# Routed blocks of an audio tower: gate and up products in banks of their own, weights applied in PSUM, 99 blocks, a pair's rows in place

## The reference

```python
fwd = ewma(x); bwd = ewma(x reversed), reversed back      # carry = 0.1 * xi + 0.9 * carry
h = (fwd + bwd) / 2 @ W.T + b                             # 12000 tokens x 256
h = h + hidden_of_two_selective_scans(layernorm(h))       # state 64: softplus, exp, h_t = d_t * h_(t-1) + g_t
x2 = layernorm(h)
shared = (silu(x2 @ Gs.T) * (x2 @ Us.T)) @ Ds.T           # hidden 512
# 16 experts in 4 groups of 4: best 2 groups by the sum of their two best scores,
# in them the best 4 experts, w = their sigmoid scores over their sum
hw = silu(x2 @ gate_e) * (x2 @ up_e) * w_e                # hidden 64 for each expert
out = h + shared + sum over e of hw @ down_e
```

## Time and profile before

| | |
|---|---|
| median of 3 runs | 1447.79 us (1443.96 to 1449.68) |
| profiled execution | 1445.21 us, its span 1443.4 |
| mean granted TensorE clock | 0.916 of full speed |
| busy: PE, weight load, DVE | 1221.5, 1036.5, 997.5 us |
| busy: ACT, POOL | 559.2, 599.7 us |
| routed products, 512 columns (L1616) | 1272 matmuls |
| DVE scalings by token weight (L1397) | 848 x 276 ns |

### The profile page before, as it was taken

One profiled execution on the slowest core, in us unless ns is written; L12 is line 12 of the kernel. 1 busy time (PEld: TensorE's weight loads), 2 busy tenths in 40 slices (PEclk: granted clock), 3 DMA queues, 4 the chain that ended last, 5 costly groups with the idle time before them and its releaser, 6 DMA issues.

```text
span 1443.4 us, 22785 instructions
## 1 busy us (share of the span) xinstructions
PE 1221.5 (85%) x6476; PEld 1036.5 (72%) x6476; DVE 997.5 (69%) x2991; ACT 559.2 (39%) x925; POOL 599.7 (42%) x442
## 2 busy tenths in 40 slices
PE   4439948996899779996799879998699979999997
PEld 3328736884788658885688658886588868888886
DVE  6785895779548875779548885588647774665553
ACT  1523613651336423551235423463236523323332
POOL 2261163155422743146332635138341553265553
PEclk9559978998899999998899978998899999999999
DMA  3601112221221112221231112212122213123330
GB/s 73 154 27 58 32 25 79 48 45 37 39 71 41 32 43 56 68 43 33 47 81 41 32 37 43 70 38 42 37 63 49 46 42 69 40 37 58 48 36 9
DMA packets 86891, 71.00 MB, mean 49 GB/s; under 512 B 38654, under 2 KB 81471, under 8 KB 86776
## 3 DMA queue, kind: packets, MB, share of 16 engines
q0 software_dynamic: 23616, 25.52, 11.6%
q1 hardware_dynamic: 60928, 43.61, 10.6%
q10 hardware_dynamic: 2232, 0.42, 0.2%
HBM read 33.10 MB, written 39.52 MB: 50 GB/s over the span
## 4 chain that ended last, share of the span: by engine, by line
PE 56%; DVE 25%; issue 10%; POOL 3%; DMA 3%; ACT 2%; POOLq 0%; DVEq 0%; SPq 0%; ACTq 0%
PE gu_ps L1616 14%; PE gu_ps L1593 13%; PE d_ps L1674 9%; PE d_ps L1656 6%; DVE hid L1397 5%; PE ch_ps L1567 3%; PE ch_ps L1511 2%; PE ch_ps L1643 2%; DVE h L1404 1%; DVE h L1137 1%; DVE fw L1038 1%; DVE states L1115 1%; PE ch_ps L1635 1%; PE ch_ps L1521 1%; DVE ends L1030 1%
## 5 line engine op out<-in xcount | busy, mean ns | idle before, releaser
L745 POOL DMA_INDIRECT out_dram<-block_rows,entry x106 | 171.7, 1620 | 328.2 <-ACT block_rows L886 173.0
L1616 PE MATMUL gu_ps<-gu_hi,bx_hi 128*128 x424 | 193.0, 455 | 12.8 <-issue 12.7
L713 POOL DMA_INDIRECT lists<-listed,pos x96 | 131.8, 1373 | 164.7 <-DVE pos L1307 140.2
L1656 PE MATMUL d_ps<-down,hid 128*125 128x256 f32 x768 | 191.6, 395 | 0.0
L1397 DVE SCALAR_TENSOR_TENSOR hid<-gu_ps,entry,hid 128x64 f32<-128x64 f32 x848 | 171.7, 276 | 8.0 <-ACT hid L873 7.1
L1616 PE MATMUL gu_ps<-gu_hi,bx_lo 128*128 x424 | 176.1, 415 | 0.0
L1616 PE MATMUL gu_ps<-gu_lo,bx_hi 128*128 x424 | 175.4, 414 | 0.0
L1656 PEld LDWEIGHTS d_ps<-down,hid 128*125 128x125 f32 x768 | 147.9, 198 | 22.8
L873 ACT ACTIVATE hid<-gu_ps 128x512 f32<-128x512 f32 x106 | 63.4, 598 | 231.9 <-PE gu_ps L1616 231.8
L734 POOL DMA_INDIRECT block_rows<-token_rows,entry x106 | 112.5, 1061 | 64.5 <-issue 35.5
L1408 DVE TENSOR_TENSOR bx_lo<-ch_ps,bx_hi 128x256 fp32r<-128x256 f32 x106 | 44.6, 421 | 131.5 <-ACT bx_hi L880 127.9
(11 more groups left out here) (273 smaller groups left out, 3006.8 us busy)
## 6 DMA issues: line engine op xcount, KB each, us to landing
token_rows<-xn SPq DMA_DIRECT2D x24, 500.0 KB
out_dram<-h SPq DMA_DIRECT2D x24, 500.0 KB
t<-rstd_scratch SPq DMA_DIRECT2D x24, 250.0 KB, 4.0
x_in<-in_x_dram SPq DMA_DIRECT2D x15, 375.0 KB, 3.4
entry<-lists SPq DMA_DIRECT2D x106, 8.0 KB, 2.5
block_rows<-token_rows,entry POOLq DMA_INDIRECT x106, 2.8
out_dram<-block_rows,entry POOLq DMA_INDIRECT x106, 3.8
lists<-listed,pos POOLq DMA_INDIRECT x96, 2.7
```

The lines of the kernel that those rows point to most:

```text
L713: pool.indirect_dma_start(out=lists, out_offset=bass.IndirectOffsetOnAxis(pos[:, arg:arg + 1], 0), in_=listed[:, arg, :], in_offset=None). ...
L745: pool.indirect_dma_start(out=out_rows[0:there, :], out_offset=bass.IndirectOffsetOnAxis(entry[n % UE][:, ID:ID + 1].bitcast(U32), 0), in_ ...
L1616: last = pe.matmul(gu_ps[:, 2 * (g % 2) + q, :], a[n % 2][:, k, :], w[:, k, bass.ds(of, 1), :].rearrange("p g h -> p (g h)"), start=(k == ...
L1656: last = pe.matmul(d_ps[0:TP, j, :], hid[g % 4][:, tc], down[:, m, :], start=(m == 0 and j % 2 == 0), stop=(m == M - 1), skip_group_check= ...
```

## The change

- Blocks: each pair gives only as many as are sure to be full (`take`), 6, 12, 12, 11, 12, 12, 12 and 22: 99. A missing one leaves its slot empty of products; the first pair with blocks has them in its last six routed slots.
- `block_products`: first the gate columns of both groups, 256 each, into one bank, then the up columns into the other. `silu` follows the first half in the same slot on ACT; PE's first half waits for `silu_done` of two slots ago, its second for `hid_done`.
- `block_hidden`: one multiplication of the up bank by the eight weights in place in PSUM (at the start of the next slot), and one of silu by that.
- `h_tok` and `h2` become two buffers that pairs take in turn, with `y` in place. Routing has a scratch of its own (`route_t`).
- The class row uses 64 partitions for each sequence with a wait between them. The exponential's table is loaded ahead of the waits in `ssm_log` and `ssm_decay`.
- New due ticks; an `EARLY` table for the first two pairs; the splitting of the routed weights due at ticks 1.4 to 11.4.

```diff
 CHAIN = (
-    ("ewma", 0, dict(SP=-32.0, DVE=-30.5, POOL=-29.0, ACT=-28.5)),
-    ("ewma_back", 0, dict(DVE=-29.5)),
-    ("ewma", 1, dict(SP=-27.5, DVE=-28.5, POOL=-27.0, ACT=-26.5)),
+    ("ewma", 0, dict(SP=-32.0, DVE=-33.5, POOL=-29.0, ACT=-28.5)),
+    ("ewma_back", 0, dict(DVE=-32.0)),
+    ("ewma", 1, dict(SP=-23.5, DVE=-28.5, POOL=-27.0, ACT=-26.5)),
...
-    ("tok", 4, dict(PE=-24.5, DVE=-24.0)),
+    ("tok", 4, dict(PE=-25.0, DVE=-25.0)),
...
-    ("ln2_stats", 2, dict(DVE=-1.0, POOL=-0.5)),
+    ("ln2_stats", 2, dict(DVE=0.5, POOL=-2.0)),
...
-    ("list", 0, dict(POOL=15.0)),
+    ("list", 0, dict(POOL=12.5)),
...
-    ("table", 2, dict(DVE=17.0)),
-    ("table", 3, dict(DVE=17.0)),
+    ("table", 2, dict(DVE=16.5)),
+    ("table", 3, dict(DVE=17.5)),
...
+EARLY = {
+    (1, "tok", 5): dict(DVE=-24.5),
+    (1, "table", 3): dict(DVE=19.5),
+    (1, "list", 11): dict(POOL=22.0),
...
 PREPARE = (
...
-    (-16.4, "routed", 0),
-    (-14.4, "routed", 1),
...
+    (1.4, "routed", 0),
+    (3.4, "routed", 1),
...
-    taken = 0
+    take, first = [0], [0]
     for q in range(1, NP):
-        taken = min(taken + KB, full(q))
-    KE = (B * T - NCLS) // P + NCLS - taken
-    NB = KB * (NP - 1) + KE
+        first.append(first[-1] + take[-1])
+        take.append(min(KB, full(q) - first[q]))
+    first.append(first[-1] + take[-1])
+    KE = (B * T - NCLS) // P + NCLS - first[NP]
+    take.append(KE)
+    NB = first[NP] + KE
+    iteration = [q for q in range(NP + 1) for _ in range(take[q])]
...
-        for n, k in enumerate(ROUTED):
-            at_tick[TICKS * q + k] = ("B", KB * (q - 1) + n) if q else ("", 0)
+        for n, k in enumerate(ROUTED, take[q] - KB):
+            at_tick[TICKS * q + k] = ("B", first[q] + n) if n >= 0 else ("", 0)
...
+        rows_of = [sb(f"h{n}", [P, NJ * D]) for n in range(2)]
+        h_of = [h[0:TP, :].rearrange("p (j d) -> p j d", d=D) for h in rows_of]
...
-        ws1 = sb("ws1", [P, 2, D])
+        ws1 = sb("ws1", [P, D])
...
+        route_t = sb("route_t", [TP, 744])
-        gpen = fw[0:TP, 0:NJ * NG]
+        gpen = route_t[0:TP, 0:NJ * NG]
...
             def store_base(pair, t):
                 wait(sp, "fin_done", 2 * (NT * pair + t + 1))
+                wait(sp, f"base_st{t}", 16 * pair)
...
                 elif step == "ssm_log":
+                    act.preload_act_table(ACT.Exp)
...
                 elif step == "ssm_decay":
+                    act.preload_act_table(ACT.Exp)
                     wait(act, "delta_done", 2 * pair + arg + 1)
...
-            def block_silu(g):
-                wait(act, "prod_mm", done(g))
+            def silu(g, n):
+                wait(act, "half_mm", done(g))
                 hidden_is_free(g)
-                inc(act.activation(hid[g % 4].rearrange("p (g h) -> p g h", g=2),
-                                   gu_ps[:, 2 * (g % 2):2 * (g % 2) + 2, 0:GH], ACT.Silu), "silu_done")
+                inc(act.activation(hid[g % 4][:, 0:n], gu_ps[:, 2 * (g % 2), 0:n], ACT.Silu), "silu_done")
...
-                if slot(g - 1)[0] == "B":
-                    block_silu(g - 1)
+                if slot(g + 1)[0] == "B":
+                    block_x(slot(g + 1)[1], g + 1)
                 if slot(g - 4)[0] == "B":
                     block_sum(slot(g - 4)[1], g - 4)
-                if slot(g + 1)[0] == "B":
-                    block_x(slot(g + 1)[1], g + 1)
                 run(before)
-                if slot(g)[0] == "S":
-                    shared_silu(g)
+                if slot(g)[0] != "":
+                    silu(g, TT if slot(g)[0] == "S" else 2 * GH)
                 run(amid)
...
                     if pair:
                         wait(dve, "ew_lo_done", 2 * pair + b)
-
-                        wait(dve, "place_mm", pair - 1)
...
                 elif step == "tok":
                     wait(dve, "tok_mm", 6 * pair + arg + 1)
-                    wait(dve, "y_ev", 6 * (pair - 1) + arg + 1)
-                    hv = h_tok[:, 2 * arg:2 * arg + 2, :]
+                    if pair == 1 and arg == 0:
+                        wait(dve, "shared_mm", 4)
+                        wait(dve, "fold_mm", 7)
+                    elif pair >= 2:
+                        wait(dve, f"base_st{arg // 2}", 16 * (pair - 1))
+                    hv = h_of[pair % 2][:, 2 * arg:2 * arg + 2, :]
...
-                    wait(dve, f"base_st{t}", 16 * pair)
...
-                    hv = h2[:, j:j + 2, :]
-                    inc(dve.tensor_tensor(hv, ch(step, arg, pair)[0:TP, :].rearrange("p (j d) -> p j d", d=D),
-                                          h_tok[:, j:j + 2, :], ALU.add), "y_ev")
+                    hv = h_of[pair % 2][:, j:j + 2, :]
+                    inc(dve.tensor_tensor(hv, ch(step, arg, pair)[0:TP, :].rearrange("p (j d) -> p j d", d=D), hv,
+                                          ALU.add), "y_ev")
...
-                    if isinstance(pair, int) and pair == NP - 1:
-                        wait(dve, "ew_lo_done", 2 * pair + (2))
-                    else:
-                        wait(dve, "ew_lo_done", 2 * pair + (4))
...
-                for e in range(2 * EG):
-                    h = hid[g % 4][:, e * H:(e + 1) * H]
-                    up = gu_ps[:, 2 * (g % 2) + e // EG, GH + e % EG * H:GH + (e % EG + 1) * H]
-                    last = dve.scalar_tensor_tensor(h, up, entry[n % UE][:, e:e + 1], h, ALU.mult, ALU.mult)
-                inc(last, "hid_done")
+                up = gu_ps[:, 2 * (g % 2) + 1, :].rearrange("p (e h) -> p e h", h=H)
+                if part == 0:
+                    wait(dve, f"entry_in{n % UE}", 16 * (n // UE + 1))
+                    wait(dve, "prod_mm", done(g))
+                    w = entry[n % UE][:, 0:2 * EG].unsqueeze(2).broadcast_to([P, 2 * EG, H])
+                    inc(dve.tensor_tensor(up, up, w, ALU.mult), "up_weighed")
+                else:
+                    h = hid[g % 4].rearrange("p (e h) -> p e h", h=H)
+                    wait(dve, "up_weighed", n + 1)
+                    wait(dve, "silu_done", done(g))
+                    inc(dve.tensor_tensor(h, h, up, ALU.mult), "hid_done")
...
+                elif slot(g - 1)[0] == "B":
+                    block_hidden(slot(g - 1)[1], g - 1, 0)
...
                     for b in range(2):
+                        own = slice(b * N, (b + 1) * N)
                         last = pe.matmul(bank[0:TP, b * D:(b + 1) * D],
-                                         t1[:, T - 1:T].broadcast_to([P, TP]), ws1[:, b, :],
+                                         t1[own, T - 1:T].broadcast_to([N, TP]), ws1[own, :],
                                          start=True, stop=True)
+                        if b == 0:
+                            inc(last, "row_half")
+                            wait(pe, "row_half", pair + 1)
...
             def banks_of_slot(g):
-
-                if slot(g)[0] == "S" and slot(g - 2)[0] == "S":
-                    wait(pe, "silu_done", done(g - 2))
-                else:
-                    wait(pe, "hid_done", done(g - 2))
+                wait(pe, "silu_done", done(g - 2))
...
                 banks_of_slot(g)
-                for q in range(2):
-                    if q:
+                for half in range(2):
+                    if half:
                         between(amid, g)
                         groups(g + 1)
-                    of = group_of[n][q]
-                    for k in range(KD):
-                        for m, (a, w) in enumerate(((bx_hi, gu_hi), (bx_lo, gu_hi), (bx_hi, gu_lo))):
-                            last = pe.matmul(gu_ps[:, 2 * (g % 2) + q, :], a[n % 2][:, k, :],
-                                             w[:, k, bass.ds(of, 1), :].rearrange("p g h -> p (g h)"),
+                        wait(pe, "hid_done", done(g - 2))
+                    for q in range(2):
+                        of = group_of[n][q]
+                        for k in range(KD):
+                            for m, (a, w) in enumerate(((bx_hi, gu_hi), (bx_lo, gu_hi), (bx_hi, gu_lo))):
+                                last = pe.matmul(gu_ps[:, 2 * (g % 2) + half, q * GH:(q + 1) * GH], a[n % 2][:, k, :],
+                                                 w[:, k, bass.ds(of, 1), half * GH:(half + 1) * GH].rearrange(
+                                                     "p g h -> p (g h)"),
...
-                    inc(last, ("half_mm", "prod_mm")[q])
+                    inc(last, ("half_mm", "prod_mm")[half])
```

More of the change, by code:

```diff
@@ new lines @@
+    ("class_row", 0, dict(PE=-7.0, DVE=-7.5)),
+    ("residual", 4, dict(POOL=-2.5)),
+    ("split", (1, 1), dict(ACT=-6.0, DVE=-7.0)),
+    ("residual", 5, dict(POOL=-2.0)),
+    ("y", (0, 0), dict(PE=-5.5, DVE=-6.0)),
+    ("y", (0, 1), dict(PE=-5.0, DVE=-4.5)),
+    ("ln2_stats", 0, dict(DVE=-4.5, POOL=-4.5)),
+    ("y", (1, 0), dict(PE=-4.5, DVE=-4.5)),
+    ("ln2_norm", 0, dict(DVE=-3.5, ACT=-3.5)),
+    ("y", (1, 1), dict(PE=-4.0, DVE=-4.0)),
```

(7 more changed lines are left out.)

254 lines of the change are left out of this document (119 added, 135 removed).

## The result

The changed kernel takes **1365.09 us** (median of 4, 1362.24 to 1368.14) against 1447.39 (4 runs, 1443.96 to 1449.68) beside it: ratio 0.9434 [0.9405, 0.9462]. The forecast was 1368, with a range of 1315 to 1425. The profiled execution took 1365.87, its span 1364.1, so 79.3 us less span than before; the prediction's sum had 79.5.

A forecast was written before the change was run, and what follows sets the result against it. TensorE bounds slots 0 to 16 of middle pairs and the last blocks; VectorE and the dependency chain bound start-up, pair 0 and slots 17 to 23. Terms sum to -79.5: 1445.2 - 79.5 + 2.6 = 1368 us, range 1315 to 1425.

The forecast's parts named there:

- Silu in its own slot: Routed blocks: silu waits for the gate half only, in its own slot of ACT's queue; no time counted, 0.
- Seven blocks: Six fewer in the first pair with blocks, one in the fourth: -21, -3 and -4.9, sum -29 us.
- Split products: Each block: twelve 512-column products become 24 of 256, +0.07 us a block, +7 us over 99 blocks.
- Rival D: Short products: each pays its 0.19 us weight load unhidden, +1.65 us a block over the forecast's, 1531 us; chance 0.02.
- Weighing: Each block: eight VectorE scalings (1.62 us) become two operations (1.37 us), -0.25 us of DVE a block.
- Slots 17 to 23: Five such stretches: 8.16 us less DVE work at 1.28 us of time per us, -10.4 each, -52 in all.
- rival A: Slots 17 to 23: PE-DVE bank handshake makes the waits, new order only moves them; 1420 us, chance 0.20.
- Rival C: Slots 17 to 23: six ACT steps queue behind the waiting silu, 2.44 us each, +88, 1456 us; chance 0.04.
- One pair before the end: The slots 17 to 23 stretch before the last pair: smaller DVE saving, less DVE-bound, -4 us.
- Slots 0 to 16: Work moved into slots 14 to 16 ahead of PE-bound work: +1.5 us a pair, +7 in all.
- Start-up -9, pair 0 +1: Start-up: moved weight splits give back 6.3, earlier Exp table 2.6; pair 0: splits +6, scans and table parts -5.
- The last pair and the tail: End of the span, last pair with the tail: +1.9 us.

The follow-up runs named there:

- blocks_only: The kernel before with only the number of routed blocks changed, 106 to 99: 1418.28 us.
- wide: The kernel after with 512-column products, gate beside up in one bank, silu at the head of the next slot, weighing as one mid-slot operation: 1346.15 us.
- old_block: The kernel after with the whole block code of the kernel before, eight scalings included; new block count, rows and due ticks stay: 1351.44 us.
- busy_17: The kernel after with one unread VectorE reduction more in each of slots 17 to 23 of pairs 1 to 5: 1368.30 us.
- last_ticks: late_silu with the due ticks of the kernel before for the last steps of a pair's chain only (from tick -8 on): 1381.31 us.
- late_silu: The kernel after with a block's silu issued at the head of the next slot, as in the kernel before: 1343.78 us.
- residual_first: late_silu with the first three GpSimd residual additions due at tick -7.0 instead of -6.5, ahead of four list scatters: 1347.11 us.

## Why the prediction was right, and where only its sum was

The time came within 3 us, and that was in part luck. The biggest wrong term, the silu at 0, cost 21 us; without it the kernel takes 1343.8, 24 us under the forecast, because the rest brought more than forecast.

- **Seven blocks, -29.** Right: -28.9 alone, 33.6 taken from the other side. Pair 1 gave more than its share (-27.0 where 24 were forecast); pair 4's 4.9 is not seen in blocks_only.
- **Split products, +0.07 a block.** Right: period 4.97 against 4.88, 0.09; 4.89 with 512 columns. Rival D is out: starts stay 0.12 apart. By the isolated gap of the Trainium skill ("TensorE: Matmul & The Clock Gate", section "Back-to-back issue gap") 256 columns would be an estimate of 109 ns, and a block 0.03 us more; the trace has 120 ns and 0.09 us, so the measured spacing decides.
- **Weighing, 1.37 us for the two.** Right: 0.70 + 0.68. In time, the eight scalings cost some 5.3 us in all (wide against old_block).
- **Slots 17 to 23, -10.4 each.** The size was right (65.1 us, forecast 65; whole pairs 2, 3 and 5 -7.7, -9.8, -9.8), the reason was not. This is the step that failed: "8.16 us less for DVE, x1.28". The slope came from comparing two stretches which differ in DVE work and also in which steps of the chain they hold. busy_17 added DVE work and nothing else and found 0.06 (pairs 2 to 5 whole) to 0.25 (their stretches). The other factor was off too, and by luck the other way: DVE's work fell by 11.3 us, not 8.2. Most of the surplus is line 1074, three operations in 3.7 us before and two in 0.3 after (line 1090), though one such operation takes 0.17 as a rule; so that part of VectorE's busy time was not work. The ticks were worth 7.3 to 7.5 us a pair in pairs 2 to 4. That they do it by changing who waits for whom fits last_ticks, whose times don't follow DVE's work, but is argued. Of rival A the waits on passed banks are there; its conclusion, that a new order can't shorten the stretches, was wrong.
- **Silu in its own slot, 0.** Wrong: +21.3. Rival C had the mechanism, a copy of x behind a silu that waits, and the delay: 2.44 us forecast, 2.35 measured (2.78 - 0.43). It priced six such steps in each stretch; the trace shows one that reaches PE, 1.9 us, and the low clock behind it. At 2 to 5 us in each of six pairs it ate a fifth of what the rest brought (21 of 104), and stayed below the 79.5 at which C decides.
- **One pair before the end, -4.** Wrong: +2.7 for the stretch, +3.8 for the pair. With the silu late it is 50.3 us and the clock 1.00 instead of 0.91. But the silu is not the only thing that lengthens it: blocks_only, with the silu of before, has 55.3 us there at a clock of 0.91. The ticks also lose 5.9 in this pair; which of them, stays open.
- **Slots 0 to 16, +1.5 a pair.** 0.9 measured for pair 3 (91.0 to 91.9); late_silu has 90.9.
- **Start-up -9, pair 0 +1.** -13.1 and +0.8. The splits' two prices were nearly confirmed; the table's 2.6 was not seen, and ticks that I had counted at nothing gave the rest.
- **The last pair and the tail, +1.9.** +7.0. 34 blocks x 0.09 are 3.1, and one wait for a gather is 3.5 us, where the kernel before has 1.0 in the same part:

```profile
PE ch_ps L1650 <- DMA block_rows<-token_rows,entry: 3.5, 1, 3.5
```

By part, then: blocks -29 to -34; ticks -41.7; the block code +13.7 with the new ticks (-7.7 banks and weighing, +21.3 silu). These are worths against different neighbours and need not sum to 82.3. At the old ticks the block code came together with the buffers and brought -11.5, so what a part is worth depends on the order around it. The two row buffers and the scratch of routing were not run alone.

The lowest median is that of the kernel after with only its silu moved back: 1343.78 us, 0.928 [0.926, 0.931] of before and 21 us below after. `wide` (1346.15) and residual_first (1347.11) can't be told from it.

## What to carry to other kernels

A price per us of work, read from two stretches that differ in more than that work, is a correlation: add dummy work to one stretch, which is cheap and tests it, before building a sum on it. When an instruction is moved forward in a strictly ordered queue, price what stands behind it while it waits, not the instruction; releasing it "as soon as its input is half there" can be worse than issuing it when it never waits. And read where a gain that came true came from: this forecast was within 0.2% and hid a removable loss of 21 us.

## What the runs showed of the hardware

- A 128x512 multiplication with PSUM in and out in the same place, the second input broadcast from SBUF, takes 0.70 us, against 0.68 for the one that writes to SBUF.
- 35 extra VectorE reductions (23.7 us) cost 2.5 to 3.2 us of time here, with intervals that overlap.
- A wait of 1.9 us on TensorE in each of six pairs cost as much again in slower matmuls: 11.6 us more idle, 11.5 us more busy for the same 5083 matmuls. In pair 3 the granted clock behind it was 0.79 over 8 us.
- A VectorE multiplication with both inputs in SBUF took 5.88 us instead of 0.94 while three additions ran on GpSimd (4.32 us, residual_first); one with a PSUM input ran inside two such additions in 0.69 (late_silu).
